# Expert tiles of a routed FFN: eight zero scatters ahead of tile 0, and tiles 1 to 4 wait by the table

## The reference

```python
xt = x.reshape(-1, 256)                         # 8192 tokens
scores = softmax(xt @ gate_w.T + gate_b)        # 8 experts
top_w, top_i = top_k(scores, 2)                 # every token goes to 2 of them
gate_dense = sum(one_hot(top_i, 8) * top_w[..., None], axis=1)
def expert(w1e, b1e, w3e, b3e, w2e, b2e):
    h = silu(xt @ w1e.T + b1e) * (xt @ w3e.T + b3e)   # 256 wide
    return h @ w2e.T + b2e
y = einsum('etd,te->td', vmap(expert)(...), gate_dense)
z = silu(xt @ ws1.T + bs1) * (xt @ ws3.T + bs3) @ ws2.T + bs2   # shared expert
out = x + layernorm(y + z)
```

## Time and profile before

| What | Value |
|---|---|
| median of three runs | 1165.63 us |
| profiled execution, its own time | 1167.16 us |
| its span, first to last instruction | 1165.3 us |
| PE busy | 998.3 us (86%) |
| DVE busy | 884.2 us (76%) |
| POOL busy | 772.7 us (66%) |
| ACT busy | 568.1 us (49%) |
| mean granted TensorE clock | 0.927 |
| scatters into sum_y (L1521) | 142, 223.5 us busy on POOL |
| weights of one tile | 514, 512 and 512 KB |
| x of one tile | 260 KB |

### The profile page before, as it was taken

The page is one execution under the profiler, slowest core; times in us unless marked ns, Lnnn a source line. Parts: engine busy times, 40 slices in busy tenths (PEclk is TensorE's granted clock), DMA queues, the critical chain, the costliest instruction groups (busy, mean ns, idle before and its releaser), DMA issues. The chain is left out here.

```text
span 1165.3 us, 23279 instructions
## 1 busy us (share of the span) xinstructions
PE 998.3 (86%) x6344; PEld 883.9 (76%) x6344; DVE 884.2 (76%) x2213; ACT 568.1 (49%) x1027; POOL 772.7 (66%) x790
## 2 busy tenths in 40 slices
PE   4658999999999999999995775969999999999452
PEld 3546878887888788878785665969999999998331
DVE  6688888998899889988986233757776777776486
ACT  4355556655665566556543432424443444444265
POOL 2355787779777877787677531457766767666498
PEclk9779999999999999999998877989999999999655
DMA  5331444344434442344232137588778878887697
GB/s 187 89 99 49 142 149 125 101 135 142 132 96 133 140 144 89 128 140 153 73 119 74 69 130 253 123 221 166 114 117 205 164 165 197 169 203 149 193 399 299
DMA packets 109813, 174.06 MB, mean 149 GB/s; under 512 B 13741, under 2 KB 77896, under 8 KB 109512
## 3 DMA queue, kind: packets, MB, share of 16 engines
q1 hardware_dynamic: 78136, 121.02, 32.5%
q0 software_dynamic: 26592, 35.67, 17.6%
q10 hardware_dynamic: 5040, 16.85, 3.8%
HBM read 173.53 MB, written 78.21 MB: 216 GB/s over the span
## 5 line engine op out<-in xcount | busy, mean ns | idle before, releaser
L1521 POOL DMA_INDIRECT sum_y<-e_y,e_row_at x142 | 223.5, 1574 | 43.9 <-issue 41.1
L1353 PE MATMUL e_h_ps<-e_z_hi,e_w 128*128 128x256 f32 x1136 | 218.1, 285 | 18.9 <-DVE e_h L1436 10.8
L1353 PEld LDWEIGHTS e_h_ps<-e_z_hi,e_w 128*128 128x128 f32 x1136 | 182.1, 192 | 22.2 <-DVE e_h L1436 11.1
L1165 POOL DMA_INDIRECT slots_x<-f_xf,f_at x128 | 138.1, 1079 | 35.5 <-issue 35.5
L1353 PE MATMUL e_h_ps<-e_z_lo,e_w 128*128 128x256 f32 x568 | 160.5, 283 | 0.0
L1397 ACT ACTIVATE e_act_h<-e_h_ps,e_w 128x256 f32<-128x256 f32 x142 | 67.3, 475 | 187.6 <-PE e_h_ps L1353 162.6
L1369 PE MATMUL e_y_ps<-e_w,e_h_hi 128*128 128x256 f32 x568 | 118.4, 292 | 1.1 <-DVE e_h_lo L1443 1.1
L574 PE MATMUL f_h_ps<-f_f_hi,f_w_hi 128*128 128x512 f32 x256 | 108.4, 423 | 6.7 <-ACT f_h_room L720 3.9
L1436 DVE SCALAR_TENSOR_TENSOR e_h<-e_h_ps,e_w,e_act_h 128x256 f32<-128x256 f32 x142 | 68.1, 483 | 60.7 <-ACT e_act_h L1397 58.5
L852 DVE RECIPROCAL f_den<-f_den 128x256 f32<-128x256 f32 (+1 forms) x48 | 109.2, 2279 | 0.6
L1353 PEld LDWEIGHTS e_h_ps<-e_z_lo,e_w 128*128 128x128 f32 x568 | 108.3, 191 | 0.0
(11 more groups left out here) (221 smaller groups left out, 2993.8 us busy)
## 6 DMA issues: line engine op xcount, KB each, us to landing
e_w<-w_split SPq DMA_DIRECT2D x71, 514.0 KB
e_w<-w_split SPq DMA_DIRECT2D x71, 512.0 KB
e_w<-w_split ACTq DMA_DIRECT2D x71, 512.0 KB
e_x_in<-slots_x SPq DMA_DIRECT2D x71, 260.0 KB
f_x_in<-x SPq DMA_DIRECT2D x16, 512.0 KB, 5.3
f_x_res<-x SPq DMA_DIRECT2D x16, 512.0 KB, 4.7
x_dram<-f_x_room SPq DMA_DIRECT2D x16, 512.0 KB, 2.9
sum_y<-f_y SPq DMA_DIRECT2D x32, 256.0 KB, 2.2
```

The source lines that it names most:

```text
L1165: pool.indirect_dma_start(out=slots_x[:, :], out_offset=bass.IndirectOffsetOnAxis(ap=at[p][:, j, k:k + 1], axis=0), in_=xf[p][:, j, :], in ...
L1353: last = pe.matmul(h_ps[q][:, which, :], w13(p, q, part)[:, which, c, :], z[p % 2][:, c, :], start=(n == 0), stop=(n == 5))
L1521: pool.indirect_dma_start(out=dst[:, :], out_offset=bass.IndirectOffsetOnAxis(ap=row_at[p][:, j:j + 1], axis=0), in_=y[p][:, j, :], in_off ...
```

## The change

Three things change. In the table, entries 1 to 4 are made like all others, so that 32 is subtracted where the expert stays the same. Counting starts later: before tile 0, POOL clears the four y buffers and sends each of them once, two scatters each, to the spare rows, so that each y_stored semaphore starts from 32 (`BEGUN`), and with the base of the table raised accordingly (land_base starts at 7 // 4 instead of 3 // 4, in units of 32) the table's counts stay positive with 32 subtracted. DVE fills the four row_at buffers with spare row numbers for it. All waits on y_stored are raised by 32; so `read_y` and `read_rows` of tiles 0 to 3 and the holds of tiles 0 and 1, which waited for nothing, now wait for the zero scatters of their buffer.

```diff
-                dve.tensor_copy(tile_of["land"][:, 0:5], land_s[:, 0:5])
+                dve.tensor_copy(tile_of["land"][:, 0:1], land_s[:, 0:1])
...
-                dve.scalar_tensor_tensor(out=tile_of["land"][:, 5:TILES], in0=same_as[:, 5:TILES],
-                                         scalar=-16.0 * (SLOT_TILE // P), in1=land_s[:, 5:TILES], op0=ALU.mult,
+                dve.scalar_tensor_tensor(out=tile_of["land"][:, 1:TILES], in0=same_as[:, 1:TILES],
+                                         scalar=-16.0 * (SLOT_TILE // P), in1=land_s[:, 1:TILES], op0=ALU.mult,
...
+        BEGUN = 16 * SUBS
+
+        def y_landed(s, p):
+            return BEGUN + landed_of_four(s, p, SUBS)
...
-                sp.wait_ge(y_stored[p], 16 * SUBS * ((tiles + 3 - p) // 4))
+                sp.wait_ge(y_stored[p], BEGUN + 16 * SUBS * ((tiles + 3 - p) // 4))
...
             dve.wait_ge(own_ready, 3)
+            for p in range(4):
+                dve.tensor_copy(row_at[p][:, :], spare_row[p % 2][:, :]).then_inc(spare_ready, 1)
...
-                wait(dve, y_stored[p], landed_of_four(s - 4, p, SUBS))
+                wait(dve, y_stored[p], y_landed(s - 4, p))
...
-                if isinstance(s, int) and s < 2:
-                    wait(pool, y_stored[before], landed_of_four(s - 1, before, SUBS))
-                else:
+                if not isinstance(s, int) or s > 0:
                     pool.wait_ge(y_stored[before], pool.value_load(tile_of["land"][0:1, bass.ds(s, 1)],
-                                                                   min_val=16 * SUBS,
-                                                                   max_val=16 * SUBS * (tiles // 4 + 1)))
+                                                                   min_val=BEGUN,
+                                                                   max_val=BEGUN + 16 * SUBS * (tiles // 4 + 1)))
                 hold(pool, scratch, held, s, (y_read, s + 1),
-                     (y_stored[(p + 2) % 4], landed_of_four(s - 2, (p + 2) % 4, SUBS)))
+                     (y_stored[(p + 2) % 4], y_landed(s - 2, (p + 2) % 4)))
+                scatter(p)
+
+            def scatter(p):
                 for j in range(SUBS):
                     pool.indirect_dma_start(out=dst[:, :], ...
...
             pool.wait_ge(scratch_ready, 1)
+            for p in range(4):
+                pool.memset(y[p][:, :, :], 0.0).then_inc(y_cleared, 1)
+            pool.wait_ge(y_cleared, 4)
+            pool.wait_ge(spare_ready, 4)
+            for p in range(4):
+                if p >= 2:
+                    pool.wait_ge(y_stored[p - 2], BEGUN)
+                scatter(p)
...
-        "land_base": (_np.arange(3, 3 + (2 * tokens + 8 * (slot_tile - 1)) // slot_tile) // 4
+        "land_base": (_np.arange(7, 7 + (2 * tokens + 8 * (slot_tile - 1)) // slot_tile) // 4
```

More of the change, by code:

```diff
@@ L1267, in expert_tiles @@
         rows_read = sem("rows_read")
+        spare_ready = sem("spare_ready")
+        y_cleared = sem("y_cleared")
         scratch_ready = sem("scratch_ready")
```

## The result

The changed kernel took 1157.82 us (median of 12 runs, 1155.04 to 1165.58) beside 1164.3 us for the kernel before (12 runs). The ratio is 0.9945, 95% interval [0.9926, 0.9963]: 6.4 us faster, between 4.3 and 8.6. In a second set of runs it was 0.9943 [0.9922, 0.9965]. The forecast was 1160.4, within 1%, with 5.2 us of gain; both that gain and the 8.3 us of rival A lie inside the interval.

What follows compares the result with a forecast made beforehand. In the expert stage, PE's pace bounds, with 12.9 us lost where late scatters meet weight loads. Terms -12.9 + 5.4 + 2.3 = -5.2 us against 1165.63 gave 1160.4; own range 1158 to 1163, whole range 1155 to 1168.

Steps and rivals of the forecast that it cites:

- rival A: Expert stage: x of tile 1 hardly delayed, weight exchanges cost what lone ones do; -8.3 us, 1157.3; chance 0.20.
- The frame: Expert tiles read alone: 12.9 us lost between DVE's row reads for tiles 5 and 17; late send meets weight loads.
- Steps 1 and 2: Table, DVE's copies and POOL's zero round before tile 0: 0 us, with 2.4 us of POOL's cover left.
- Step 3: DVE's row reads for tiles 0 to 3 now wait for zero-round landings: taken at 0, upper bound 1.7 us.
- rival C: Start of expert stage: the zero round itself is late, from landings over 8 us; +4.6 us, 1170.2; chance 0.09.
- Step 4: Zero round's scatters delay x of tile 1 on the DMA engines: 2.3 us, bounds 0 and 5.5.
- Step 5: Tiles 1 to 4 no longer wait for the tile before: the whole 12.9 us lost in rows 5 to 17 goes.
- step 6: Weight exchanges at tiles 8 and 11 still collide with scatters: 5.4 us come back, bounds 4.6 and 8.0.
- rows 5 to 17 in under 60 us: Rival A's sign: DVE's row reads from tile 5 to tile 17 take under 60 us; the forecast said about 61.6.
- no idle PE between 745 and 765: Expert stage, a sign that the forecast is right: PE has no idle time from 745 to 765 us.
- B: Expert stage: collision only moved, stage waits for weights instead; -1.5 or +0.6 us, 1164 to 1166; chance 0.19.
- D: Expert stage: the change does not act, because tiles 1 to 4 change experts after all; 1168; chance 0.02.

## Why the prediction was right

The sign, the place and most of the mechanism were right. The size was less sharp than it looks: the measured 1157.82 lies within the whole range of 1155 to 1168, but 0.2 under the forecast's own 1158 to 1163, and nearer to rival A's 1157.3. Of the 2.6 us between forecast and result 1.3 are the yardstick (1165.63 for three runs, 1164.3 for twelve).

**The frame** (the stage by itself, 12.9 us lost between rows 5 and 17, late send meets loads) held. Without the four waits the loss is 3.4 to 4.0; with them and without the loads it is 3.7; with neither it is none.

**Steps 1 and 2** (table, copies, POOL). They cost nothing, as said, but with a mistake that happened not to matter: the landings in the round took 6.2 and 8.1 us, not 4.0, so the round's own waits were not met ahead but cost POOL 3.1 us. POOL ended 19.6 us behind the start where I had 17.8. The cover of 2.4 us was still there (2.38), because y of tile 0 came 1.8 us later too.

**Step 3** (DVE's new wait). Row 0 did not wait. The third pair was released at 724.75, so the first pair had landed 1.5 us ahead of row 0 at 726.24, the margin that was worked out. The second pair, at 8.1 us, even passed the 8 us from which rival C was to count, and it cost nothing. That the two errors (later landing, later row) cancel is luck; the run with the later round shows what lies behind: 6.33 us of wait.

**Step 4** (x of tile 1). 2.3 us were expected, and 1.6 measured in both traces, at the named place. The mechanism is right by the runs with smaller and later rounds; the way to the number (two whole scatters ahead) is not, since 64 rows cost no more than 16. The loads behind x were taken to cost nothing. That was not quite so: rows 0 to 5 took 24.03 to 25.01 us in the eight traces with a round of 128 rows and 23.97 to 24.13 in the three without a round, so the round costs between 0 and 1.0 us there as well (smaller rounds took 23.80 to 24.02). The Trainium skill ("DMA: Bandwidth & Descriptors", section "Queues, rings and completion order") says that a DMA engine takes turns between the queues that have work for it, a packet at a time. The 3.4 us that the prediction made of that is not what this case shows, with 1.6; no run here shows the turns themselves.

**Step 5** (-12.9) is the step that carries the result, and it held in its path: no send of tiles 1 to 4 waits for a scatter, the waits of rows 6 and 7 are gone, and so is the clock of 0.50. One part was mis-sized. Tile 4 was to land 4 to 6 us after its last scatter began, and took 8.1, so row 8 still waited 1.67 us (1.77 in the second trace), which was to go. The predicted slack of 2.2 us covers that, and PE shows no wait for h there. The 12.9 can't be measured apart from step 6: together they were to be -7.5 and were -8.9 and -9.8 in the two pairs of traces.

**Step 6** was the term with the largest error: 5.4 taken, 3.4 to 4.0 measured, below even the lower bound of 4.6 that two lone exchanges gave. That bound was none: in the changed kernel's two traces the exchange within rows 32 to 40 cost 1.6 us (39.02) and 3.9 (41.31), so the 2.3 of one trace was no firm price. (The 37.5 that it is counted from is firm: without loads these rows took 37.46 and 37.47.) The upper bound, 8.0, left no scatter to be put off. Some were, though by less than the three tiles that I allowed: tile 8 went out at 780.49, 3.9 us behind row 10 (776.56), because it had to wait for tile 7 to land (780.49 - 773.35 = 7.1 us), and tile 12 at 798.83, 2.4 behind row 14 (796.47). The DMA engines reached 93%.

With the measured terms the sum is -12.9 + 4.0 + 1.6 + 0.1 (rows 0 to 5: 24.16 for 24.06) = -7.2; the timed runs say -6.4, between -4.3 and -8.6. Of the rivals, A (nearly all comes in) was nearest in the exchanges, but not in the start; its sign, rows 5 to 17 in under 60 us, stood in the second trace (59.63) and not in the first (60.20). The sign of no idle PE between 745 and 765 failed in a small way: counted from row 5, PE's 1.17 us for weights lie in that stretch. B is refuted by how small PE's waits for weights are, 1.8 us in all, C by row 0 and D by POOL's sends.

## What to carry to other kernels

A wait that looks cheap for each tile can decide when its debt falls due: price it not by its own length but by what the late transfer meets, here the next weight load. A transfer that only serves to raise a count should be small (the traces give 1.7 to 2.4 us for that here, the timed runs don't settle it) and lie where nothing waits for the same engines; ask of it, too, which step of the other engines now waits for its landing. And before two profiles are compared, cut them at instructions that both have: 3 to 4 us of the difference in span here were of parts that nobody had changed.

## What the runs showed of the hardware that was not expected

The time to make a scatter on POOL depends little on its rows: 1.27 to 1.35 us for 16 rows in nearly all cases, 1.39 to 1.46 for 64, 1.56 for 128. Its landing depends on them a little more, and far more on what the other queues do: the second pair of the zero round (with 16 rows, its last scatter begun at 719.18, it released the fourth at 725.81) took 6.6 to 6.9 us with 16 rows, 7.5 with 64 and 8.1 with 128, where a scatter of 128 rows takes 4.0 in the median of the stage. Beside the weight loads tile 4's 128 rows took 8.1 to 9.5 us, without them 4.1. And x of tile 1, 260 KB, was delayed by 0.3 to 0.6 us by scatters of either 16 or 64 rows, but by 1.3 to 1.7 by scatters of 128 begun ahead of it.
